# A five-layer gated graph network on one core: tiles in groups of 4, 4, 4, 4, every first state transposed by TensorE, and the last step of a tile in two units

## The reference

```python
A = (adj != 0)
h = relu(layernorm(x))                        # the first state
for l in range(5):
    m = einsum('bnd,de->bne', h, weight[l])
    agg = einsum('bij,bid->bjd', A, m)
    gi = agg @ w_ih.T + b_ih ;  gh = h @ w_hh.T + b_hh
    r = sigmoid(i_r + h_r) ;  z = sigmoid(i_z + h_z)
    n = tanh(i_n + r * h_n)
    h = (1 - z) * n + z * h
out = x + h * nodemask
```

## Time and profile before

| what | us |
|---|---|
| median of 3 runs | 381.57 |
| lowest, highest | 380.69, 382.64 |
| the profiled execution's own time | 382.65 |
| its span | 380.9 |
| granted TensorE clock, mean | 0.99 of full |
| PE busy | 366.4 |
| VectorE busy | 313.4 |
| ScalarE busy | 297.1 |
| GpSimd busy | 277.8 |

### The profile page before, as it was taken

The page is one execution under the profiler, slowest core; times in us unless marked ns, Lnnn a source line. Parts: engine busy times, 40 slices in busy tenths (PEclk is TensorE's granted clock), DMA queues, the critical chain, the costliest instruction groups (busy, mean ns, idle before and its releaser), DMA issues.

```text
span 380.9 us, 6557 instructions
## 1 busy us (share of the span) xinstructions
PE 366.4 (96%) x2160; PEld 185.5 (49%) x2160; DVE 313.4 (82%) x574; ACT 297.1 (78%) x490; POOL 277.8 (73%) x261
## 2 busy tenths in 40 slices
PE   7769999999999999999999999999999999999992
PEld 3335555555555545445454545544455555555541
DVE  4794889888877879998989989887977778777785
ACT  3975889989878889798888978778767777677663
POOL 3555797797797889968685876757876655555796
PEclk9998999999999999999999999999999999999997
DMA  7836256387453844745285593407833432296422
GB/s 221 215 35 138 53 115 139 59 190 146 115 156 83 167 91 105 151 100 112 55 157 121 104 190 96 110 18 159 160 81 83 96 73 55 55 222 176 102 83 83
DMA packets 114128, 44.46 MB, mean 117 GB/s; under 512 B 91168, under 2 KB 107808, under 8 KB 114096
## 3 DMA queue, kind: packets, MB, share of 16 engines
q1 hardware_dynamic: 113856, 43.73, 52.4%
q10 hardware_dynamic: 144, 0.26, 0.2%
q0 software_dynamic: 96, 0.07, 0.1%
HBM read 17.57 MB, written 4.19 MB: 57 GB/s over the span
## 4 chain that ended last, share of the span: by engine, by line
PE 84%; DVE 7%; DMA 3%; POOL 2%; ACT 2%; issue 1%; SPq 0%; DVEq 0%; POOLq 0%; ACTq 0%
PE ps_r L270 9%; PE ps_r L271 8%; PE ps_z L270 8%; PE ps_r L272 8%; PE ps_z L271 8%; PE ps_z L272 8%; PE ps_s L341 4%; PE ps_s L340 4%; PE ps_in L272 4%; PE ps_in L271 4%; PE ps_in L270 4%; PE ps_hn L272 4%; PE ps_hn L270 4%; PE ps_hn L271 4%; DMA fold_in<-in_fold_lhs 1%
## 5 line engine op out<-in xcount | busy, mean ns | idle before, releaser
L747 POOL TENSOR_TENSOR zh<-z,h 128x512 f32<-128x512 f32 x80 | 101.6, 1270 | 81.3 <-ACT z L452 81.0
L446 ACT ACTIVATE r<-ps_r,b_sum,unscale 128x512 f32<-128x512 f32 x80 | 62.2, 778 | 51.1 <-PE ps_r L272 50.4
L577 DVE SCALAR_TENSOR_TENSOR rhn<-ps_hn,b_hn,r 128x512 f32<-128x512 f32 x80 | 60.0, 750 | 19.7 <-ACT r L446 19.4
L456 ACT ACTIVATE ps_in<-ps_in,b_ih,unscale 128x512 f32<-128x512 f32 x80 | 60.0, 750 | 19.0 <-DVE ps_in L583 17.2
L752 POOL TENSOR_TENSOR hp<-h,hp 128x512 f16<-128x512 f32 x64 | 74.4, 1162 | 0.0
L583 DVE TENSOR_TENSOR ps_in<-ps_in,rhn 128x512 f32<-128x512 f32 x80 | 56.0, 700 | 16.7 <-PE ps_in L272 14.6
L589 DVE SCALAR_TENSOR_TENSOR ps_in<-z,ps_in 128x512 f32<-128x512 f32 x79 | 54.6, 691 | 11.0 <-ACT ps_in L456 11.0
L452 ACT ACTIVATE z<-ps_z,b_sum,unscale 128x512 f32<-128x512 f32 x80 | 61.6, 770 | 1.0 <-PE ps_z L272 1.0
L594 DVE TENSOR_TENSOR h<-zh,ps_in 128x512 f32<-128x512 f32 x78 | 53.6, 688 | 9.7 <-POOL zh L747 1.9
L571 DVE TENSOR_TENSOR s_lo<-ps_s,s_hi 128x512 f16<-128x512 f32 x80 | 54.4, 681 | 0.0
L440 ACT CAST s_hi<-ps_s 128x512 f16<-128x512 f32 x80 | 46.6, 583 | 0.7
(11 more groups left out here) (109 smaller groups left out, 751.6 us busy)
## 6 DMA issues: line engine op xcount, KB each, us to landing
x_in<-in_x SPq DMA_DIRECT2D x16, 256.0 KB, 4.5
adj_in<-in_adj SPq DMA_DIRECT2D x16, 256.0 KB, 4.3
x_out<-in_xT SPq DMA_DIRECT2D x16, 256.0 KB, 3.0
mask_in<-in_mask_row SPq DMA_DIRECT2D x16, 256.0 KB, 3.7
out<-x_out SPq DMA_DIRECT2D x15, 256.0 KB, 2.3
nat<-hp SPq DMA_TRANSPOSE x64, 3.1
fold_in<-in_fold_lhs SPq DMA_DIRECT2D x1, 320.0 KB, 5.5
out<-x_out ACTq DMA_DIRECT2D x1, 256.0 KB, 2.6
```

The source lines that it names most:

```text
L446: nc.scalar.activation(r[:], ps_r[:], ACT.Sigmoid, bias=b_sum[:, 0:1], scale=unscale[:, 0:1]).then_inc(r_done, 1)
L456: nc.scalar.activation(ps_in[K % 2][:], ps_in[K % 2][:], ACT.Tanh, bias=b_ih[:, 2:3], scale=unscale[:, 0:1]).then_inc(n_done, 1)
L577: nc.vector.scalar_tensor_tensor(out=rhn[:], in0=ps_hn[:], scalar=b_hn[:, 0:1], in1=r[:], op0=ALU.add, op1=ALU.mult).then_inc(rhn_done, 1)
L747: nc.gpsimd.tensor_tensor(zh[:, K % 2], z[:, K % 2], h[:, t % RING], ALU.mult).then_inc(zh_done, 1)
```

## The change

There are four groups of four tiles in place of 4, 6 and 6. With them the units of tiles 4 to 15 move, and with these the units of their preparation and of their last step; the rules for `prep` and `ends` stay as they are. Tile 4's preparation starts at unit 5 in place of unit 1, that of tiles 9, 10 and 15 at 24, 29 and 54 in place of 16, 21 and 46. Tiles 8 to 15 are now five units apart in it.

All tiles from 4 on take the way through `ps_t`; the planes, their DMA transposes and the joins are gone.

The multiplication by the mask and the addition of a tile are two functions now. The addition comes one unit after the multiplication, except where another tile ends in that next unit or the program is about to end (tiles 12 to 14). The store follows the addition by a unit. `FINISH` goes from 5 to 3.

```diff
-GROUPS = (4, 6, 6)
+GROUPS = (4, 4, 4, 4)
...
-HALVES = 10
 FETCH = 6
-FINISH = 5
+FINISH = 3
...
+    adds = {t: ends[t] + (ends[t] + 1 not in ending and ends[t] + 2 < N) for t in ends}
+    adding = {adds[t]: t for t in ends if t < TILES - 2}
+    storing = {adds[t] + 1: t for t in ends}
     fetching = {ends[t] - FETCH: [t] for t in ends}
-    fetching[N - FINISH - FETCH].append(TILES - 1)
+    fetching.setdefault(N - FINISH - FETCH, []).append(TILES - 1)
...
                 if K in tile_at_stage[6]:
                     transpose_first(tile_at_stage[6][K])
-                    if tile_at_stage[6][K] >= HALVES:
-                        transpose_halves(tile_at_stage[6][K])
-                if K - 1 in ending:
-                    store(ending[K - 1])
+                if K in storing:
+                    store(storing[K])
...
-                if tile_at_stage[5].get(K, HALVES) < HALVES:
+                if K in tile_at_stage[5]:
                     transpose_first(tile_at_stage[5][K])
                 aggregate(K + 1)
...
-                if K in tile_at_stage[6] and tile_at_stage[6][K] < HALVES:
+                if K in tile_at_stage[6]:
                     transposed(tile_at_stage[6][K])
-                if K in tile_at_stage[6] and tile_at_stage[6][K] >= HALVES:
-                    split(tile_at_stage[6][K])
...
-                if tile_at_stage[8].get(K, 0) >= HALVES:
-                    join(tile_at_stage[8][K])
...
+            def masked_result(t):
+                f = t % FRING
+                pool.wait_ge(ends_loaded[f], 32 * (t // FRING + 1))
+                pool.wait_ge(h_done, at[t, LAST] + 1)
+                nc.gpsimd.tensor_tensor(mask_in[:, f], mask_in[:, f], h[:, t % RING], ALU.mult).then_inc(masked, 1)
+
             def final(t):
                 f = t % FRING
                 if t < TILES - 2:
-                    pool.wait_ge(ends_loaded[f], 32 * (t // FRING + 1))
-                    pool.wait_ge(h_done, at[t, LAST] + 1)
-                    nc.gpsimd.tensor_tensor(mask_in[:, f], mask_in[:, f], h[:, t % RING], ALU.mult).then_inc(masked, 1)
                     pool.wait_ge(masked, t + 1)
...
                 if K in ending and K < N - 1:
-                    final(ending[K])
+                    masked_result(ending[K])
+                if K in adding:
+                    final(adding[K])
```

More of the change, by code:

```diff
@@ L11 @@
 I32 = mybir.dt.int32
-U16 = mybir.dt.uint16
 P = 128
@@ L122, in gnn_kernel @@
         nat = ctx.enter_context(nc.sbuf_tensor("nat", [P, RING, 2 * TG, P], F16))
-        halves = ctx.enter_context(nc.sbuf_tensor("halves", [P, 2, 2, TILE], U16))
-        halves_t = ctx.enter_context(nc.sbuf_tensor("halves_t", [P, 2, 2 * TG, P], U16))
         s_hi = sb("s_hi", [P, 2, TILE], F16)
@@ L142, in gnn_kernel @@
         ends_loaded = [sem(f"ends_loaded{i}") for i in range(FRING)]
-        halves_loaded = [sem(f"halves_loaded{i}") for i in range(2)]
         stored = [sem(f"stored{i}") for i in range(FRING)]
@@ L157, in gnn_kernel @@
         nat_hi_init, nat_lo_init = sem("nat_hi_init"), sem("nat_lo_init")
-        split_done = sem("split_done")
         h_hi_init, h_lo_init, h_init = sem("h_hi_init"), sem("h_lo_init"), sem("h_init")
@@ L210, in transpose_first @@
                 sp.dma_start_transpose(hp[:, t % RING], pair(nat, t)).then_inc(hp_loaded[t % RING], 16)
[L212 to L217, removed]
             def transpose(K):
@@ L405, in layernorm @@
                     act.wait_ge(nat_lo_init, t - LN + 1)
-                    act.wait_ge(t_mm, min(t - LN + 1, HALVES))
+                    act.wait_ge(t_mm, t - LN + 1)
                 for q in (2 * half, 2 * half + 1):
@@ L428, in transposed @@
                 nc.scalar.activation(h[:, t % RING], ps_t[:], ACT.Relu).then_inc(h_init, 1)
[L430 to L436, removed]
             def s_high(K):
@@ L620, in last_result @@
                 nc.vector.tensor_tensor(x_out[:, f], x_out[:, f], ps_in[K % 2][:], ALU.subtract).then_inc(last_out, 1)
[L622 to L627, removed]
             def v_low(l):
```

## The result

The changed kernel takes 383.33 us (median of 16 runs, 382.0 to 386.13), the one before 381.06 us beside it (16 runs, 380.49 to 382.88). The ratio is 1.0055 with a 95% interval of 1.0041 to 1.0069, so 1.6 to 2.6 us slower. The forecast was 382.6 us and "within 0.5%". The time lies in the range given, the direction is the one forecast, and the size was about half of what came.

The account below looks back on a forecast made before the run. PE was taken as the bound, busy 96% of the span. +2.64 - 1.9 + 0.2 + 0.15 = +1.1 us on the 381.57 us median gave 382.6 us ("same", within 0.5%), range 380.8 to 384.9.

Parts of the forecast that it names:

- PE transposes, +2.64: On PE, six more tiles transposed at 0.44 us each, with nothing to hide them under: +2.64 us.
- All 1.9 us of pauses go: PE's waits for VectorE's `s_lo` from unit 20 to 79 vanish without joins and long GpSimd units: -1.9 us.
- Groups of four, +0.2: Two units less from a state to its next layer; late GpSimd plus slow landing may pause PE: +0.2 us, bounds 0 and 4.
- The 2.1 us of spare time: Time left between a state's `nat` transpose landing and its next aggregation, down from 10.7 us with two units less.
- the first rival: PE waits at aggregations for `nat` not landed, 1.0 us at three places: +3 us, 385.6 us; chance 0.13.
- End, +0.15: Tile 15's mask moves from unit 75 to 77, delaying GpSimd's last pieces: +0.15 us, bounds 0 and 0.7.
- The sum, +1.1: Whole kernel: +2.64 - 1.9 + 0.2 + 0.15 us, with 0 for the start.
- the start's rival: Units 1 and 2: shorter wait for the first `hp` and fewer slow products (some 16), 380.9 or 378.9 us; chance 0.07.
- The way back: From a state to its next layer: PE waits at aggregations for late `nat`, +3 us, 385.6 us; chance 0.13.
- The pauses did not stay: Rival: preparation statistics and GpSimd's units keep `s_lo` late, only 0.7 of 1.9 us gone, 383.9 us; chance 0.10.
- the sign that was named for it: Unit 4's aggregation starting earlier than 37.4 us would show that the start got shorter.
- the full record of a transpose: Rival: on PE, new transposes cost 24 x 0.27 us a row's full records, +6.5 - 2.64, 386.5 us; chance 0.02.

Follow-up runs that it names:

- e4: Changed kernel with groups put back to (4, 6, 6) and FINISH = 5; ratio 1.0036 to the kernel before.
- e1: Kernel before with HALVES = 16, so PE also transposes the first states of tiles 10 to 15; ratio 1.0047.
- e2: Kernel before with only a tile's last step put in two units, mask then addition, store a unit later; ratio 0.9977.
- e8: Changed kernel with FETCH = 5 in place of 6, moving the loads for a tile's end; not timed, stretch from unit 4 to 79 333.00 us.
- e6: Changed kernel (groups of four) with the edit of e5, VectorE adding the fp16 pair in place of PE transposes from tile 4 on; ratio 0.9999.
- e5: e4 without PE transposes of first states from tile 4 on, VectorE adding the fp16 pair in stage 8; ratio 0.9951 to the kernel before.
- e7: e5 with the fp16 pair added by scalar_tensor_tensor in place of tensor_tensor; ratio 0.9934 to the kernel before.
- e9: e5 with GpSimd in place of VectorE adding the pair for tiles 10 to 15; 377.96 us, ratio 0.9906 to the kernel before.
- b3: Changed kernel, unedited, for a second profile; stretch from unit 4 to 79 332.37 us.

## Why the prediction came out as it did

**PE transposes, +2.64: right.** A unit with `ps_t` is 4.77 us, twelve times, as said beforehand. In the stretch of e4 against before, once 1.96 us of pauses are taken off, 2.62 us are left.

**All 1.9 us of pauses go: right.** None is left. The division (1.3 behind joins, 0.6 behind long GpSimd units) is borne out by e1 and e2. The `zh` behind unit 26 is 1.2 us late (146.57), near the 1.3 forecast; the latest ones, behind units 21 and 41, are 1.5 us late, which the forecast had not found. VectorE's `s_lo` did not suffer.

**Groups of four, +0.2: the mechanism right, the size 0.37.** Unit 11's transfers did it as named. The other place, unit 44's transpose, I had not foreseen; an instruction packet isn't in the order of instructions. The 2.1 us of spare time are borne out (unit 66's transpose: 2.1), and unit 41's, behind the latest GpSimd unit, had 0.9 us left, unit 26's 1.4. That a late issue and a slow landing must meet for a pause held as well: unit 11's transpose was issued 0.5 us late, because SP had two more loads to issue ahead of it, and landed after 5.2 us; unit 44's was 0.3 us late, because the split-off addition on GpSimd stood ahead of `zh` and the low part, and landed after 5.0 us. Without the lateness neither would have made PE wait. The pauses were 0.14 and 0.23 us and not the 1.0 us of the first rival, since GpSimd was late by 0.3 us at most in them and not by 1.3.

**End, +0.15: 0.24.** In the rows that answer to the earlier trace rows, VectorE's last instruction now waits for GpSimd's sum:

```profile
375.48 1.27 POOL L748 TENSOR_TENSOR x_out<-x_out,zh 128x512 f32<-128x512 f32 x1
...
376.85 0.69 DVE L599 TENSOR_TENSOR x_out<-x_out,ps_in 128x512 f32<-128x512 f32 x1 [0.22 <-POOL x_out L748]
```

The end is 12.29 or 12.30 us in all five profiles with FINISH = 3 and 12.04 to 12.07 in all nine with FINISH = 5.

**The sum, +1.1: its terms came to 1.3, the runs to 1.6 to 2.6.** The four terms are right within 0.2 us; what the sum lacked lies outside them, 0.9 us on the mean of the runs. That the time came near the forecast is in part luck: the 381.57 us it started from, a median of three runs, were 0.5 us above the 381.06 of sixteen, and this covered half of what was missing. The sum put nothing in two places.

First, the time around the span: I carried it over unchanged. It is 1.79 to 1.82 us in all nine profiles of kernels in which PE does not transpose every tile, 2.00 to 2.01 in e1, e4 and e8, and 2.16 in both of the changed kernel. The spans of the other executions say more: 1.75 to 1.85 us in 68 executions of the kernel before, 1.96 to 2.05 in the 16 of e1 and e4, and in the 16 of the changed kernel 1.95 to 3.38, with a mean of 2.32. That is +0.2 us with the transposes and +0.5 on the mean with the whole change. What it consists of, the profile can't show.

Second, the start. The 16 spans of the changed kernel have a mean of 381.16 us, the 68 of the kernel before 379.7 (379.5 to 379.9 by batch). The difference is 1.2 to 1.6 us, and 1.3 of it is stretch and end. So 0 to 0.3 us are left for the start, or for waits for `nat` that other executions had and the two profiled ones had not. Unit 4's aggregation, at 36.10 and 37.06 us against 35.33, 36.89 and 37.41, is too scattered to decide this: a clock dip comes or stays away in either kernel. With 0.5 us outside the span the account closes to within 0.4 us of the 2.2 us between the means of the runs; this rest stays open.

The baseline was off as well: the profiled execution of before had the dip and stood at the upper end of its runs. Its span was no measure of the usual run; only the stretch behind the start was. And the dip was counted too large in the start's rival: it is eight products at 0.43 us, 1.7 us, not some 16. That it "follows from" the wait for `hp` isn't borne out either: a wait for `hp` stands there in all fourteen profiles, a dip in seven.

**Rivals.** The way back did get too long, but for 0.4 us and not for 3. The pauses did not stay. Nothing shows that the start got shorter by the change: 36.10 us is earlier than 37.4, the sign that was named for it, but the kernel before has been at 35.33 itself. PE does not pay the full record of a transpose: e4's 0.44 us a tile against 1.1.

## What to carry to other kernels

When one engine is saturated, count only what is put on it and what its pauses are worth: here six transposes (2.6 us) could at best be paid for by 1.9 us of pauses, and this was visible before anything ran. Ask next whether the work is needed there at all; the state was already in place as an fp16 pair, and one addition in place of all transposes and joins from tile 4 on, for half of the tiles on the engine with room, made the kernel 1% faster, together with the last step in two units (0.5 us in e2). The price is a first state of two fp16 parts in place of the full fp32 one. And compare stretches between two fixed points of the program rather than spans, when the start differs from one execution to the next.

## What the runs showed of the hardware that I had not expected

- A VectorE addition of two fp16 operands in SBUF (128 x 512) takes 0.68 us when no GpSimd instruction is running (e6) and up to 1.67 us when one is, 1.36 and 1.39 at the mean by either instruction (e5, e7); GpSimd's next one, where it follows at once, took 1.57 us (e6) and 1.61 (e5) in place of 1.16. GpSimd does the same addition in 1.16 us (e9).
- Packets with instructions (16 KB) come 16 times behind unit 4, 13 of them at places that repeat to 0.6 us from profile to profile (changed, b3). One beside three transfers of the kernel went with a landing of 5.0 us where 3.2 was seen without it (changed, e8); one alone seldom did anything (52 of 55 landings within 3.6 us).
- The steady part repeats to 0.02 us in three profiles of the kernel before, while the start varies by 2.1 us, with and without eight products at half of PE's clock in unit 2.
- The time outside the span is 1.75 to 1.85 us in 68 executions of the kernel before, 1.96 to 2.05 in 16 of e1 and e4, and 1.95 to 3.38 in 16 of the changed kernel.
